# Three query products of the self-attention put between the transposes of the normed tiles, and one expert's low part taken off the way to the first attention tile

## The reference, cut to what matters

```python
x = x + cross_attention(layernorm(x), ctx)      # 32 x 257 context rows, 8 heads
h = layernorm(x)
Q = sigmoid(4 * (batchnorm(h @ Wq) - 1)); K, V likewise with Wk, Wv
t_Q = 1 - mean(Q);  t_K = 1 - mean(K)           # one number for each token
A = where(t_Q - t_K < 0, f, -f) + 0.9           # f = 0.9 * exp(-|t_Q - t_K| / 0.5)
x = x + A @ V @ Wo + bo
x = x + mixture_of_8_experts(layernorm(x))      # top 2, w1, w3, w2 of each expert
```

## Time and profile before

| | |
|---|---|
| median of 3 runs | 747.01 us (745.41 to 749.55) |
| the profiled execution | 746.17 us, its span 744.4 us |
| PE busy | 715.5 us |
| DVE busy | 492.6 us |
| ACT busy | 441.5 us |
| POOL busy | 238.4 us |
| mean granted clock of TensorE | 0.997 of full speed |

### The profile page before, as it was taken

One profiled execution on the slowest core, in us unless ns is written; L12 is line 12 of the kernel. 1 busy time (PEld: TensorE's weight loads), 2 busy tenths in 40 slices (PEclk: granted clock), 3 DMA queues, 4 the chain that ended last, 5 costly groups with the idle time before them and its releaser, 6 DMA issues.

```text
span 744.4 us, 14155 instructions
## 1 busy us (share of the span) xinstructions
PE 715.5 (96%) x4910; PEld 593.7 (80%) x4910; DVE 492.6 (66%) x904; ACT 441.5 (59%) x958; POOL 238.4 (32%) x207
## 2 busy tenths in 40 slices
PE   4899999999999999999999999999999979999996
PEld 3677888888888888888888888788778857788875
DVE  6766776775766757756667676967467875755573
ACT  4655776675766757756757565564655435556560
POOL 1462211221211212121212142753840023555534
PEclk9999999999999999999999999999999999999999
DMA  9931121212121212112212304631115457655659
GB/s 302 105 129 42 44 87 44 85 42 85 42 85 42 85 42 81 46 55 72 84 43 82 103 2 151 206 118 51 58 35 195 137 172 249 108 103 109 112 73 337
DMA packets 59672, 75.21 MB, mean 101 GB/s; under 512 B 8784, under 2 KB 33360, under 8 KB 59632
## 3 DMA queue, kind: packets, MB, share of 16 engines
q1 hardware_dynamic: 52032, 58.16, 26.0%
q0 software_dynamic: 4720, 11.27, 8.3%
q10 hardware_dynamic: 2880, 5.24, 2.0%
HBM read 54.75 MB, written 19.92 MB: 100 GB/s over the span
## 4 chain that ended last, share of the span: by engine, by line
PE 85%; DVE 7%; DMA 3%; ACT 3%; issue 2%; SPq 0%; POOL 0%; DVEq 0%; POOLq 0%; ACTq 0%
PE pK L32 42%; PE pV L32 11%; PE pP L32 9%; PE pV L1643 5%; PE pT L1544 4%; PE pT L1735 4%; PE pS L1687 2%; PE pP L1717 2%; DMA fin<-total 1%; PE pT L1882 1%; PE pT L1524 1%; PE pS L1812 1%; DMA total<-big,idx 1%; PE pS L1905 1%; DVE bst L1001 1%
## 5 line engine op out<-in xcount | busy, mean ns | idle before, releaser
L32 PE MATMUL pK<-parts 128*128 128x512 f32 x744 | 187.7, 399 | 0.0
L540 POOL TENSOR_TENSOR parts<-big,parts 128x1024 fp32r<-128x1024 f32 x32 | 77.9, 2435 | 309.5 <-ACT parts L767 309.5
L32 PEld LDWEIGHTS pK<-parts 128*128 128x128 f32 x744 | 134.4, 188 | 27.0 <-issue 1.2
L1043 DVE TENSOR_TENSOR kn<-pK,head_rs 128x512 f32<-128x512 f32 x62 | 42.9, 692 | 58.1 <-ACT head_rs L681 58.1
L32 PE MATMUL pK<-w,lhs 128*128 x276 | 69.1, 399 | 1.0 <-issue 0.6
L32 PEld LDWEIGHTS pK<-w,lhs 128*128 128x128 f32 x276 | 50.3, 188 | 12.4 <-issue 2.8
L1464 DVE TENSOR_TENSOR w_p<-big,w_p 128x1024 fp32r<-128x1024 f32 x22 | 27.0, 1226 | 37.8 <-ACT w_p L958 37.8
L32 PE MATMUL pP<-pT,parts 128*128 128x256 f32 x384 | 51.8, 284 | 0.1
L615 POOL DMA_INDIRECT big<-x_rows,idx_x x23 | 26.7, 1162 | 73.6 <-DVE idx_x L1420 59.4
L1037 DVE TENSOR_REDUCE head_ss<-sq 128x8 f32<-128x512 f32 x62 | 42.5, 685 | 11.5 <-ACT sq L675 11.5
L675 ACT ACTIVATE sq<-pK 128x512 f32<-128x512 f32 x62 | 36.8, 594 | 21.5 <-PE pK L32 21.4
(11 more groups left out here) (331 smaller groups left out, 1528.9 us busy)
## 6 DMA issues: line engine op xcount, KB each, us to landing
big<-in_ctx_dram SPq DMA_DIRECT2D x32, 512.0 KB, 3.8
total<-zero SPq DMA_DIRECT2D x32, 256.0 KB, 4.0
w_raw<-in_L_ffn_w_dram SPq DMA_DIRECT2D x16, 512.0 KB, 5.8
big<-in_L_ffn_w_dram SPq DMA_DIRECT2D x8, 512.0 KB, 4.3
fin<-total SPq DMA_DIRECT2D x8, 512.0 KB, 8.1
x_rows<-big ACTq DMA_DIRECT2D x8, 256.0 KB, 2.1
total<-big ACTq DMA_DIRECT2D x8, 256.0 KB, 2.3
big<-in_x_dram SPq DMA_DIRECT2D x1, 1536.0 KB, 10.4
```

Of the source, the lines that this page charges most:

```text
L32: last = pe.matmul(out, lhs(a, c), rhs(b, c), start=start and c == first and n == 0, stop=stop and c == chunks - 1 and n == 2)
L540: nc.gpsimd.tensor_tensor(ctxN[:, u, LO], ctx_raw[:, u], ctxN[:, u, HI].bitcast(F32), ALU.subtract).then_inc(cn_lo, 1)
L1043: tt(heads(kn[:, t]), heads(pKV[t][:, :]), per_head(head_rs[:, t]), ALU.mult).then_inc(k_n, 1)
```

## The change

```diff
@@ -901,7 +901,7 @@                                   (ACT)
                 if n == 3 * TILES - 4:
                     w13_high(3)
-                if n == 3 * TILES - 2:
+                if n == 3 * TILES - 3:
                     self_high(0)
@@ -1294,8 +1294,6 @@                                 (DVE)
                 if n == 3 * TILES - 2:
-                    w13_low(3)
-                if n == 3 * TILES - 1:
                     self_low(0)
                 dve.wait_ge(z_mm, n + 1)
@@ -1365,6 +1363,8 @@                                 (DVE, the output's loop)
                 if s + 1 < TILES:
                     self_low(s + 1)
+                if s < 2:
+                    w13_low(3, slice(2 * s, 2 * s + 2))
                 if s == TILES:
                     token_rows(0)
@@ -1768,11 +1768,11 @@                               (PE)
             for t in range(TILES):
+                if 4 <= t < TILES - 1:
+                    z_product(t - 4)
                 ln_turn(TILES + t)
                 if t + 5 < TILES:
                     project(t + 5)
-                elif t >= 5:
-                    z_product(t - 5)
@@ -1885,7 +1885,7 @@                                 (PE)
                 if j == 0:
-                    pe.wait_ge(w13_lo, 4 + 2 * C)
+                    pe.wait_ge(w13_lo, 5 + 2 * C)
```

## The result

| | median | runs |
|---|---|---|
| before | 746.07 us (745.41 to 749.55) | 20 |
| changed | 748.86 us (747.07 to 751.16) | 20 |
| ratio | 1.0032, 95% interval 1.0022 to 1.0041 | |

The change costs 0.32% or 2.4 us: within the 0.5% that was called "no change", but more than the +0.9 us of the forecast. The forecast's 747.9 stood on a median of three runs, 747.01; of twenty it is 746.07, so 747.0 would have been the same forecast on this scale. The time lies inside the range of 745.0 to 750.4.

What follows compares the result with a forecast made beforehand. The prediction took PE, busy 96% of 744.4 us, as the bound, so its standstills count in full. It summed +2.2 - 1.3 = +0.9 us to 747.9 us on the median's scale, range 745.0 to 750.4.

Steps and rivals of the forecast that it cites:

- The moved steps start without a wait, and the wait for tile 3's low part goes: Self-attention head: query products between PE's turns start without a gap, removing PE's 1.29 us wait.
- The standstill ahead of `z_product(3)`: Self-attention head: tile 6's later turn delays `z_c(0)`; PE stands still some 3.8 us and `z_product(3)` starts 2.2 us late.
- Part B: Passage to the output: the first attention tile's low part comes sooner, so PE's 1.26 us wait goes, -1.3 us.
- The clock stays: Self-attention head: the granted clock stays at 1.00 from 494 to 502 despite the new gap, costing nothing.
- the first rival: Self-attention head: the clock falls to 0.50 in the new gap for 3.4 us, total +2.3 us, 749.3; chance 0.30.
- the forecast's own case: Whole kernel: longer standstill at the head, output wait gone, clock unchanged; +0.9 us, 747.9 us; chance 0.45.
- The rival's price: Dense products after the new gap: 3.4 us at half clock lose 1.4 us; chance of the clock falling 0.30.
- The sum: Whole kernel: +2.2 us at the self-attention head and -1.3 us at the passage to the output give +0.9 us.
- The chain does not bind: Rival at the self-attention head: `z_product(3)` is not held up, both old waits go, -2.6 us, 744.4; chance 0.12.
- part B gives nothing: Rival at the passage to the output: something else holds the first output product, +2.2 us, 749.2; chance 0.08.

Runs made afterwards that it cites:

- part B alone: Kernel before with only the passage to the output changed (ACT's first attention copy earlier, expert 3's low part in the output loop): 0.9988 of the time before.
- part A alone: Kernel before with only PE's new order of turns and query products at the head of the self-attention: 1.0048 of the time before.

## Why the prediction was right, and where it was not

- **The moved steps start without a wait, and the wait for tile 3's low part goes.** Right: the starts are within 0.11 us of those worked out.
- **The standstill ahead of `z_product(3)`, +2.2 us.** Right in place, cause and size: 2.25 us late. The bracket's 3.57 us are fewer than the 3.8 of the sum since it counts from the modelled end of the turns, 491.56 + 1.04 = 492.60, and not from 492.3; taking `z_c(0)` out of the chain takes the whole of it away. The table load counts 1.28 us in it: the copy behind starts 0.01 us after it ends, and moving it out shortened the wait by 1.3 us. The 1.38 us of drain that the Trainium skill (ScalarE: Activation LUTs, What ACT_TABLE_LOAD costs) puts on top of a load was not seen.
- **Part B, -1.3 us.** Right, a little small: -1.5 us in the trace (-0.9 by the ratio of part B alone, 0.2 to 1.6). The two halves of expert 3's low part cost nothing. What I described as one cause was two in series.
- **The clock stays.** This is the step that failed: the sum put the clock at nothing, and it cost 2.1 us as a mean. "Against: dense products stand on both sides of it, and the 1.29 us gap here left the clock alone" weighed too much. In all three profiles with the 3.6 us gap (changed kernel twice, part A alone) the clock fell. It was the first rival, 0.30, that came true; the forecast's own case is seen, by the mean clocks, in two of the twenty executions.
- **The rival's price, +1.4 us.** Right in kind; 1.6 and 1.7 us where the half level lasted about 3.4 us, but 2.9 us in the execution where it lasted 6.8, and 2.1 us as a mean. Two things made it small. The price of a microsecond was 0.42 us where 0.47 is right: the ten matmuls of the earlier trace rows start at 599.30 and the clock falls near 599.9, so their 0.41 us each is a mean over both levels, where at half level one takes 0.43; and 0.237 is a little more than the 0.23 of dense matmuls. With 0.47 the same 3.4 us give 1.6, as measured. And the length was taken from a single place, where the profiled execution of the changed kernel had twice as much.
- **The sum.** +2.2 - 1.3 with the clock's mean 2.1 is +3.0 us with the terms of the prediction, and 2.25 - 1.5 + 2.1 = +2.9 with the measured ones, against +2.4 (1.6 to 3.1) by the ratio. The 2.1 us are themselves a difference of two such ratios, so this is a check within 1 us and no proof. The range held the time and the sign was right, but not by the forecast's own case: the range was wide enough for a term of 2 us that the sum had left out, and "within 0.5%" held because that term is small against the kernel.
- **"The chain does not bind" and "part B gives nothing"** are both refuted by the wait and by part B alone.

## What to carry to other kernels

Before work is moved ahead of a step on a full engine, follow what the displaced step feeds, through every other engine's list, to the next wait on the full one; here four transposes put 4.1 us later stood at the head of a chain of five instructions, and a 1.3 us wait became one of 3.6. The cure was not to undo the move but to take the one instruction that was waited for out from behind the chain. A standstill of TensorE among dense matmuls can cost more than its own length (here 2.1 us more as a mean behind one of 3.6 us, where one of 1.3 us left the clock alone), and a profile of one execution does not say how much: where times scatter and one profile looks too good for the median, take another.

## What was not expected of the hardware

The granted clock fell to 0.50 in two of three profiled executions behind a standstill of 2.3 us with eight transposes ahead of it and dense products on both sides of these, and in three of three behind 3.6 us; by the mean clocks, two of the twenty timed executions of the changed kernel very likely had no fall. With the same instructions and the same 3.6 us it stayed there for 3.4 us once and for 6.8 us once. With 9 or 15 matmuls in the standstill it stayed at 1.00, in one profile of each. What decides between executions of one kernel was not settled.
